# A recurrent two-stage kernel: the loop over batches is divided inside the scan, ten states after its start

## The reference, cut to what matters

```python
xn = layernorm(x)
s  = scan_forward(xn) + scan_backward(xn)       # 2 directions x 16 states
g  = silu(moe_ffn(xn))                          # gelu FFN 128-512-128, times top-2 router weight
x  = x + s * g                                  # stage A ends here: x1
xn = layernorm(x)
s  = mamba2(xn)                                 # rope, rmsnorm, conv of 4 taps, 4 heads, chunked SSD, gated norm
g  = silu(local_transformer(xn))                # 2 layers: window attention (8 heads, 64), then a gelu FFN
x  = x + s * g                                  # x2, the output
# the scan, per direction and state s:
#   h[t] = exp(delta[t] * A[s]) * h[t-1] + delta[t] * B[s, t] * xn[t];   y += C[s, t] * h[t]
```

## Time and profile before

| | us |
|---|---|
| three timed runs | 4567.24 (median), 4563.26, 4567.44 |
| the profiled execution | 4559.8 |
| its span, first to last instruction | 4557.9 |
| granted TensorE clock, mean, as a share of the full one | 0.905 |
| PE busy | 3514.9 (77%) |
| DVE busy | 2834.3 (62%) |
| ACT busy | 2303.5 (51%) |
| POOL busy | 1720.2 (38%) |
| scans, L1157, 512 | 625.0 |
| POOL's idle time ahead of L1391, waiting for scans | 1686.1 |
| DMA, mean | 4 GB/s over the span |

### The profile page before, as it was taken

How to read it: one execution, slowest core, us unless ns; L and a number is a source line. 1 busy time by engine, 2 the same in 40 slices (tenths; PEclk the granted TensorE clock), 3 DMA queues, 4 the chain that set the end, 5 groups by cost and what they waited for, 6 DMA issues and landing times. The chain is left out here.

```text
span 4557.9 us, 53699 instructions
## 1 busy us (share of the span) xinstructions
PE 3514.9 (77%) x16064; PEld 1913.2 (42%) x16160; DVE 2834.3 (62%) x4751; ACT 2303.5 (51%) x4006; POOL 1720.2 (38%) x1428
## 2 busy tenths in 40 slices
PE   5777777877778777787777877778787787878776
PEld 1344444444434444344443444434444343444443
DVE  6475665756657566565665657566575665756644
ACT  4454555545455555455554545455554554545444
POOL 2252442525325253342533415244252442525332
PEclk9898998989989898998999989898898998989999
DMA  1000000000000000000000000000000000000000
GB/s 76 3 1 1 5 1 5 1 1 5 1 6 1 1 5 1 6 1 6 1 1 6 1 6 1 1 6 1 6 1 1 6 1 6 1 1 3 1 3 3
DMA packets 18378, 20.44 MB, mean 4 GB/s; under 512 B 768, under 2 KB 17152, under 8 KB 17792
## 3 DMA queue, kind: packets, MB, share of 16 engines
q1 hardware_dynamic: 18048, 16.44, 1.1%
HBM read 12.24 MB, written 4.19 MB: 4 GB/s over the span
## 5 line engine op out<-in xcount | busy, mean ns | idle before, releaser
L1391 POOL TENSOR_TENSOR hc<-hst,Cs 128x512 f32<-128x512 f32 x512 | 650.2, 1270 | 1701.6 <-DVE hst L1157 1686.1
L1157 DVE TENSOR_TENSOR_SCAN hst<-dA,bank 128x512 f32<-128x512 f32 x512 | 625.0, 1221 | 267.6 <-issue 93.6
L518 PE MATMUL bank<-W,xs 128*128 128x512 f32 x960 | 477.3, 622 | 125.8 <-DVE tmp L1297 123.5
L494 PE MATMUL bank<-hc,C 128*128 128x512 f32 x1024 | 562.5, 633 | 0.8 <-POOL hc L1391 0.7
L506 PE MATMUL bank<-parts,sel 96*128 96x512 bf16 x1024 | 361.5, 408 | 222.7 <-DVE hst L1157 195.2
L1149 DVE TENSOR_TENSOR bank<-u,bank 128x512 f32<-128x512 f32 x512 | 351.6, 687 | 269.1 <-PE bank L506 239.4
L868 ACT COPY Cs<-bank 128x512 f32<-128x512 f32 x512 | 295.1, 576 | 346.6 <-PE bank L506 346.0
L1467 POOL TENSOR_TENSOR Pm<-Pm,rinv 128x512 f32<-128x512 f32 x256 | 266.5, 1041 | 480.4 <-DVE rinv L1313 467.2
L1452 POOL TENSOR_TENSOR oT<-tmp 128x512 f32<-128x512 f32 x256 | 324.7, 1268 | 322.8 <-PE bank L670 161.6
L987 ACT ACTIVATE Pm<-Pm 128x512 f32<-128x512 f32 x256 | 161.7, 632 | 461.3 <-DVE Pm L1322 461.3
L862 ACT ACTIVATE dA<-delta,neg_a 128x512 f32<-128x512 f32 x512 | 368.3, 719 | 4.3 <-issue 3.5
(11 more groups left out here) (222 smaller groups left out, 6252.5 us busy)
## 6 DMA issues: line engine op xcount, KB each, us to landing
W<-wpack SPq DMA_DIRECT2D x1, 4498.0 KB, 13.8
x_tok<-x SPq DMA_DIRECT2D x16, 256.0 KB, 3.0
out<-xa SPq DMA_DIRECT2D x16, 256.0 KB, 2.2
rot<-tables SPq DMA_DIRECT2D x2, 512.0 KB, 16.5
wc_f<-taps SPq DMA_DIRECT2D x1, 1024.0 KB, 19.9
C<-cpack SPq DMA_DIRECT2D x1, 721.0 KB, 15.0
Pm<-mask SPq DMA_DIRECT2D x1, 320.0 KB, 15.3
tmp<-rowpack SPq DMA_DIRECT2D x1, 256.0 KB, 17.7
```

Source lines behind the costliest of these rows:

```text
L494: mm(y_acc[:, :], ident, hc[:, k % 2, :], start=(k == 0), stop=(k == 2 * NS - 1))\
L518: mm(b[:, :], weights, rhs, start=True, stop=True).then_inc(full(ring, job), 1)
L1157: v.tensor_tensor_scan(o, a, b, 0.0, ALU.mult, ALU.add).then_inc(sem("a_h"), 1)
L1391: g_.tensor_tensor(hc[:, k % 2, :], hst[:, k % 2, :], Cs[:, k % 2, :], ALU.mult)\
```

## The change

Stage A's scan is cut after state 9. `scan` takes a range of states; a step now runs states 10 to 31 and the head of batch i, then the prologue and states 0 to 9 of batch i+1. `PACE` is drawn anew, so that A_END and the head start in layer 0's feed-forward, the next prologue begins one slot earlier beside layer 1's attention, and the ten states stand beside layer 1's feed-forward and the end of stage B. B's slots are as before. Batch 0's first states, and batch 1's first ten, run before the first interleaved step. After g2's Silu `tables()` loads the set of Exp and Ln. On POOL a wait for its own last prologue instruction replaces the carrying over of `prior`.

```diff
+CUT = 10
 SCAN = 0
-A_END = SCAN + 2 * NS
+A_END = SCAN + 2 * NS - CUT
 HEAD = A_END + 1
 PRO = HEAD + 8
-A_SLOTS = PRO + 9
+SCAN1 = PRO + 9
+A_SLOTS = SCAN1 + CUT
...
-PACE = [(0, 2), (LAYER, 16), (LAYER + UNITS_END, 28), (LAYER + LAYER_SLOTS, HEAD), (LAYER + LAYER_SLOTS + 5, PRO),
-        (LAYER + LAYER_SLOTS + UNITS_END, A_SLOTS - 1), (B_END, A_SLOTS - 1), (B_SLOTS, A_SLOTS)]
+PACE = [(0, 1), (LAYER, 10), (LAYER + UNITS_END, A_END), (LAYER + LAYER_SLOTS, HEAD + 5), (LAYER + LAYER_SLOTS + 4, PRO),
+        (LAYER + LAYER_SLOTS + UNITS_END, SCAN1), (B_SLOTS, A_SLOTS)]
+
+def scan_slot(k):
+    return SCAN1 + k if k < CUT else SCAN + k - CUT
...
-            alone(chain(prologue(0), scan(0), head(0), prologue(1)))
-            both(chain(scan(1), head(1), prologue(2)), stage_b(0, None))
-            both(chain(scan(2), head(2), prologue(3)), stage_b(1, 0))
+            def ready(i):
+                return chain(prologue(i), scan(i, 0, CUT))
+
+            def body(i):
+                return chain(scan(i, CUT, 2 * NS), head(i))
+
+            alone(chain(ready(0), body(0), ready(1)))
+            both(chain(body(1), ready(2)), stage_b(0, None))
+            both(chain(body(2), ready(3)), stage_b(1, 0))
             with e.Fori(3, NB - 1) as i:
-                both(chain(scan(i), head(i), prologue(e.snap(i + 1))), stage_b(e.snap(i - 1), e.snap(i - 2)))
-            both(chain(scan(NB - 1), head(NB - 1)), stage_b(NB - 2, NB - 3))
+                both(chain(body(i), ready(e.snap(i + 1))), stage_b(e.snap(i - 1), e.snap(i - 2)))
+            both(body(NB - 1), stage_b(NB - 2, NB - 3))
...
@@ scalar, stage_b
                 yield B_END
                 act.wait_ge(*step("f_y", i))
                 f(tmp2[:, 0, :], yB[:, :], ACT.Silu).then_inc(sem("g2"), 1)
+                tables()
...
@@ gpsimd, prologue
-                prior.append(step("a_parts", i))
+                pool.wait_ge(*step("a_parts", i))
```

More of the change, by code:

```diff
@@ L378, in prologue, with scan @@
                 sp.dma_start(x_tok[:, :, :], src).then_inc(sem("load"), 16)
-            def scan(i):
-                yield A_END
+            def scan(i, lo, hi):
+                yield scan_slot(lo)
             def head(i):
@@ L495, in accumulate @@
                         .then_inc(sem("a_yacc"), 1)
[L497 to L500, removed]
+                yield scan_slot(lo)
+                if lo == 0:
+                    pe.wait_ge(*step("a_parts", i))
+                for k in range(lo, hi):
+                    yield scan_slot(k)
                     d, s = k // NS, k % NS
@@ L509, in scan @@
                         accumulate(k - 2)
-                yield A_END
-                accumulate(2 * NS - 2)
-                accumulate(2 * NS - 1)
+                if hi == 2 * NS:
+                    yield A_END
+                    accumulate(2 * NS - 2)
+                    accumulate(2 * NS - 1)
             def norm_sum(ring, job, i, weights, rhs):
@@ L853, in prologue, with scan @@
                 tables()
[L855 to L859, removed]
+            def scan(i, lo, hi):
+                yield scan_slot(lo)
+                if lo == 0:
+                    act.wait_ge(*step("a_delta", i))
+                for k in range(lo, hi):
+                    yield scan_slot(k)
                     if k >= 2:
@@ L1139, in prologue, with scan @@
                                        op0=ALU.add, op1=ALU.mult).then_inc(sem("a_fo"), 1)
[L1141 to L1145, removed]
+            def scan(i, lo, hi):
+                yield scan_slot(lo)
+                if lo == 0:
+                    dve.wait_ge(*step("a_u", i))
+                for k in range(lo, hi):
+                    yield scan_slot(k)
                     d = k // NS
@@ L1157, in scan @@
                     v.tensor_tensor_scan(o, a, b, 0.0, ALU.mult, ALU.add).then_inc(sem("a_h"), 1)
[L1158 to L1168, removed]
+                if hi == 2 * NS:
+                    yield A_END
+                    dve.wait_ge(*step("a_yacc", i))
+                    v.scalar_tensor_tensor(out=ys[:, :], in0=xn[:, :], scalar=dsum[:, 0:1], in1=y_acc[:, :],
+                                           op0=ALU.mult, op1=ALU.add).then_inc(sem("a_y"), 1)
+                    dve.wait_ge(*step("a_y", i))
+                    dve.wait_ge(*step("a_gate", i))
+                    v.tensor_tensor(ys[:, :], ys[:, :], gate[:, :], ALU.mult).then_inc(sem("a_yg"), 1)
+                    dve.wait_ge(*step("a_yg", i))
+                    if later(i):
+                        dve.wait_ge(*before("m_x1b", i))
+                    v.tensor_tensor(x1[:, :], xT[:, :], ys[:, :], ALU.add).then_inc(sem("a_x1"), 1)
             def head(i):
@@ L1378, in prologue, with scan @@
                     .then_inc(sem("a_parts"), 1)
-                prior.append(step("a_parts", i))
[L1381 to L1384, removed]
+                pool.wait_ge(*step("a_parts", i))
+            def scan(i, lo, hi):
+                if lo:
+                    prior.clear()
+                for k in range(lo, hi):
+                    yield scan_slot(k)
                     pool.wait_ge(*step("a_h", i, k + 1))
@@ L1395, in head @@
             def head(i):
-                prior.clear()
                 yield HEAD + 2
```

## The result

| | before | after |
|---|---|---|
| timed runs, median | 4565.25 (4561.88 to 4567.44) | 4495.84 (4491.94 to 4501.13) |
| ratio to before, 95% interval | | 0.9849 [0.9832, 0.9866] |
| profiled execution | 4559.8 | 4495.45 |
| its span | 4557.9 | 4493.6 |
| granted TensorE clock, mean | 0.905 | 0.913 |

The changed kernel is 1.5% faster. The forecast was 4516, in a range of 4435 to 4595.

The account below looks back on a forecast made before the run. No engine is full, so the order of work within a step bounds the kernel. Steps of -4.0 us times 14, -12.7 for the last and +17.0 at the start sum to -51.7; with 7.4 for the median, 4516 us, range 4435 to 4595.

Parts of the forecast that it names:

- the 7.4 added for the median: Whole kernel: timed median before was 7.4 us above the profiled execution, so 7.4 was added to the 4508.1 sum.
- (a): Layer 1's feed-forward, wo matmuls to B's last addition: states placed beside it cost +1.8 us per step.
- (b): From B's last addition to the next step's first state-space operation: more states there cost +7.4 us per step.
- (c): State-space stage and the start of layer 0's attention: fewer states there save 7.3 us per step.
- (d): Layer 0's feed-forward and layer 1's projections: the head's layer norm overlaps the layer's, -5.4 us per step.
- (e): Layer 1's units: prologue one slot earlier, its last operations out from before wo, -0.5 us per step.
- start, once: Before the first interleaved step: nine more states run without B at 1.89 us each, +17.0 us.
- last step with A; B alone after it: Last step interleaving stage A lacks the added feed-forward and end-of-B costs, -12.7 us; no change given for B alone.
- The doubled slot: Slot 48 in layer 1's feed-forward holds two states; fg/fa matmuls start 3.1 us later than hn would let them.
- DVE needs 1.9 per state in the end block whatever the clock: Between B's last addition and the next step: each state takes DVE 1.9 us, so a higher clock would not help.
- The slower rival: Layer 0's feed-forward: head and layer chains merely follow each other, no gain there, 4597 us in all; chance 0.18.

Follow-up runs that it names:

- experiments 2 and 5: Changed kernel with the scan cut after state 4, not 9: 4461.8 us (2); that kernel with no slot holding two states: 4437.9 us (5).
- Experiment 7: Changed kernel with four more matmuls, results unused, in each of states 5 to 7: 4497.6 us, ratio to before 0.9856.
- Experiment 10: Scan cut after seven states, one state per slot, head's fifth part one slot later, against the same with five states: 4422.0 us, ratio to before 0.969.
- head late: Changed kernel with only the head put back beside layer 1's projections: 4618.8 us, ratio to before 1.0125.
- experiment 8: Changed kernel with the head's fifth part (mdt and two small DVE operations) one slot later, behind layer 1's first projection: 4444.1 us, ratio to before 0.9727.
- experiment 9: Changed kernel with the scan cut after five states, one state per slot, and the head's fifth part one slot later: 4392.4 us, ratio to before 0.9615.

## Why the prediction was right, point by point

The mechanism and the sign of each of its parts held. The time was 20 us under the forecast: the terms were off by 12.6 together, and the 7.4 added for the median did not come (the new kernel's profiled execution lies 0.4 from its median). Per full step:

| term | predicted | measured | its bounds |
|---|---|---|---|
| (a) layer 1's feed-forward | +1.8 | +3.1 | -0.5 to +5 |
| (b) end block | +7.4 | +9.2 | +6.4 to +11 |
| (c) state-space stage, attention's start | -7.3 | -9.4 | -5.8 to -10 |
| (d) head beside layer 0's feed-forward | -5.4 | -5.0 | 0 to -9 |
| (e) units | -0.5 | -3.3 | -3 to +2 |
| start, once | +17.0 | +21.7 | |
| last step with A; B alone after it | -12.7; 0 | -13.8; +3.3 | |

**(a)** The doubled slot was the right place to look, and 3.1 for it was too little. It held the feed-forward's matmuls back by 15.15 - 11.18 = 4.0, since the accumulation in it ran at the lower clock (1.92). A stage without it takes 22.0 (experiments 2 and 5).

**(b)** The step that failed is "DVE needs 1.9 per state in the end block whatever the clock". It held for two of the three states behind x2. For the third, PE at the lower of its two levels, 1.2 GHz (accumulations of 1.92) was late with its B matmul: scans 2.95 apart, +1.1. The wait for the decay matrices behind state 10 (1.09, where the earlier trace rows have 0.57) had no term either. The loop's end held DVE 1.93, less than the 2.6 said. Experiment 7 limits what the clock is worth: without the slow matmuls the wait at the loop's end and the matmuls behind it take most of it back. Experiment 10 gives the price to use, 3.3 a state. The loop's end itself can be read in the steps: the unrolled ones have an end block of 15.4 to 15.8, those in the hardware loop 17.9 to 19.2; before, 7.0 and 8.9 to 9.1.

**(c)** Right in kind. In SSD1 a state is worth 2.6, not 2.0 (29.5 with six, 26.9 to 27.1 with five, 24.3 with four): my 2.0 was the mean over six against B alone, and the sixth is not as cheap as the first. The second part gave -1.8 (-1.4 said), the attention -2.4 (-1.9).

**(d)** The best of the terms. The first projection was to start 27.5 after wo and did at 26.5; the stretch took 58.2, predicted 57.4. The slower rival, that the two chains merely follow each other, is refuted: the stretch is 5.0 shorter than before, and head late is 8.0 worse in it. What I did see in the order, mdt ahead of the projection, I took as given. It was worth 2.9 at the projection's start and 3.2 in the stretch (experiment 8). (By the prediction's own terms the step breaks even at a (d) of -1.4; the -2 said there is where the whole time does.)

**(e)** Outside its bounds, and not by the mechanism. The units' time has levels that go with the granted clock: before, 47.4 at 0.89 and 49.1 at 0.85; in the variants 48.6 at 0.86, 46.8 at 0.89, 45.3 at 0.92 to 0.96. Where the levels are nearly alike (49.1 and 48.6, 47.4 and 46.8) the gain is 0.5 to 0.6, as predicted, and the other 2.8 go with the clock, which in this stage was 0.92 or more in 13 of the 14 steps after, and 0.79 to 0.89 in all 14 before. Why stays open. The experiments exclude some causes: the units are nearly as short with the head late (46.0), without the cut (45.8) and with the gate's Silu moved back (45.8). All eleven new orders start the prologue one slot earlier, and that was not tried by itself. The same kernel has both levels in neighbouring steps (experiment 9: 45.5 and 48.6), and no experiment set the level at will.

**Start.** Batch 1's first scan came 3.7 later than before (192.67; 189.00 in the kernel before), and from there nine more states took 18.0, 2.0 each, for the 1.89 of batch 0. The 3.7 aren't the change's: the order up to there is the same, batch 0's first scan was already 3.0 later (72.34 for 69.33), and over the twelve profiles batch 1's first scan lies between 188.5 and 195.9. Rows of the kernel after; the first two gaps of 1.85 are DVE's pace, the next two rows show waits for PE:

```profile
192.67 1.22 DVE L1174 TENSOR_TENSOR_SCAN hst<-dA,bank 128x512 f32<-128x512 f32 x1 [2.48 <-ACT dA L877]
...
194.52 1.22 DVE L1174 TENSOR_TENSOR_SCAN hst<-dA,bank 128x512 f32<-128x512 f32 x1
...
198.58 0.70 DVE L1166 TENSOR_TENSOR bank<-u,bank 128x512 f32<-128x512 f32 x1 [0.99 <-PE bank L519]
...
200.93 0.70 DVE L1166 TENSOR_TENSOR bank<-u,bank 128x512 f32<-128x512 f32 x1 [0.40 <-PE bank L519]
...
214.34 1.90 DVE L1247 TENSOR_SCALAR oT<-bank,acs 128x128 f32<-128x128 f32 x7 [0.39 <-PE bank L582]
```

So the sum came out near because errors of both signs met: the costs (a), (b) and the start (spread over 14 steps) were put 1.3, 1.8 and 0.3 a step too low and the gain (d) 0.4 too high, the gains (c) and (e) 2.1 and 2.8 too low. The last of these goes with the clock, which the prediction had no term for. That it fell on the side that cancels the costs was luck: without its 2.8 a step the time would have been, an estimate, some 39 us higher, about 4535, and the forecast 19 too low. So part of the near hit is luck; the mechanism of (a) to (d) is not.

## What to carry to other kernels

When two chains are interleaved in one written order, price an item by what the slot it goes to already waits for: beside a chain of waits (a layer norm between matmuls) it is free, in a stretch that is dense or has nothing else it costs its own chain. Avoid putting two items of a chain that runs over several engines into one slot: the second one holds the other chain's work until the first is through, 4.0 to 4.4 us here in the feed-forward and the state-space stage as a whole (1.6 in two slots of its second part), against 0 in a feed-forward, 1.1 in the attention, 2.6 in the dense first part of the state-space stage and 3.3 in the end block for a single one. And after such a move look for the first instruction of the other chain that stands behind a wait that it doesn't need: one PACE number (experiment 8) gave 1.1% more.

## What was not expected of the hardware

- Some 280 matmuls of a unit stage kept PE busy 35.78 us at a granted clock of 0.96 and 39.70 at 0.86, and the stage took 45.5 and 48.6; the levels changed from step to step within one execution.
- Raising the clock in one stretch (0.72 to 0.90) moved the loss behind it: PE's issue time at the loop's end went from 1.02 to 2.32, and the accumulation behind that from 1.02 to 1.85.
- Taking 29 table loads of 1.28 us out gained nothing (4506.2 against 4495.8): they lay where ACT had room. No drain showed beside a load.
- With nothing of A beside it, layer 1's feed-forward took 23.9 at a granted 0.79; with five states in it, 22.0 at 1.00.
